# Where the second edge pass makes the own part of a message, and which banks it uses

## The reference, cut to what matters

```
def f(W1, W2, W3):
    tp = (x_src[:, :, None] * edge_sh[:, None, :]).reshape(n_edges, d * s)
    out1 = jnp.concatenate([x_src, tp], axis=-1)
    out2 = _mlp(edge_inv, W1, W2, W3)
    return out1 * out2
...
edge_v = f(Wv1, Wv2, Wv3)
edge_v = edge_v.reshape(n_edges, H, F // H) * jnp.sqrt(jax.nn.relu(alpha))[:, :, None]
node_out = jax.ops.segment_sum(edge_v, edge_dst, num_segments=n_nodes)
return node_out @ W_out
```

## Time and profile before

| | us |
|---|---|
| median of 3 runs | 4718.47 (4709.61 to 4720.08) |
| the profiled execution, its own time | 4691.75 |
| its span, first to last instruction | 4690.0 |
| busy, PE / DVE / ACT / POOL | 3424.4 / 3775.0 / 2138.1 / 1853.7 |
| granted TensorE clock, mean over the span | 0.885 |

### The profile page before, as it was taken

One profiled execution on the slowest core, in us unless ns is written; L12 is line 12 of the kernel. 1 busy time (PEld: TensorE's weight loads), 2 busy tenths in 40 slices (PEclk: granted clock), 3 DMA queues, 4 the chain that ended last, 5 costly groups with the idle time before them and its releaser, 6 DMA issues. The chain is left out here.

```text
span 4690.0 us, 65792 instructions
## 1 busy us (share of the span) xinstructions
PE 3424.4 (73%) x20105; PEld 1508.5 (32%) x20105; DVE 3775.0 (80%) x6298; ACT 2138.1 (46%) x4386; POOL 1853.7 (40%) x3682
## 2 busy tenths in 40 slices
PE   5665653465688888888888089999999999248157
PEld 2111111111233343333333034444444444112122
DVE  8999995898566666666666878888888888599898
ACT  6999991674233333333333033444434443047066
POOL 0100445000655555555554056666666666200000
PEclk9989885677899999999999589999999999579589
DMA  4754999663344444444443023333333333356445
GB/s 174 303 223 162 313 326 317 219 210 113 99 120 116 113 115 113 115 113 112 117 114 104 4 78 94 91 93 93 91 94 91 93 93 88 127 176 227 158 177 184
DMA packets 373210, 675.89 MB, mean 144 GB/s; under 512 B 74684, under 2 KB 274940, under 8 KB 361216
## 3 DMA queue, kind: packets, MB, share of 16 engines
q1 hardware_dynamic: 308752, 569.80, 37.0%
q0 software_dynamic: 39568, 78.78, 6.8%
q10 hardware_dynamic: 24544, 23.10, 1.7%
HBM read 399.80 MB, written 271.65 MB: 143 GB/s over the span
## 5 line engine op out<-in xcount | busy, mean ns | idle before, releaser
L734 POOL DMA_INDIRECT arena<-h_table,srci x808 | 772.5, 956 | 596.3 <-issue 244.2
L1751 DVE TENSOR_TENSOR arena<-banks,arena 128x1024 f32<-128x1024 f32 x404 | 493.6, 1222 | 262.9 <-remote 162.9
L829 PE MATMUL banks<-arena 128*128 128x500 bf16 x1440 | 411.4, 416 | 273.9 <-DVE arena L1474 211.4
L1871 DVE TENSOR_TENSOR arena<-banks,arena 128x512 f32<-128x512 f32 x808 | 518.8, 684 | 36.5 <-PE banks L1036 13.0
L1879 DVE TENSOR_TENSOR arena<-banks,arena 128x512 f32<-128x512 f32 x808 | 516.9, 681 | 1.3 <-PE banks L1042 1.3
L1166 ACT ACTIVATE arena<-arena,h 128x128 bf16<-128x128 f16 x1440 | 465.1, 416 | 61.0 <-DVEq L1390 40.9
L1318 ACT ACTIVATE arena<-banks 64x256 f32<-64x256 f32 x808 | 306.3, 379 | 341.2 <-PE banks L1068 334.2
L931 PE MATMUL banks<-arena 128*64 128x256 f32 x3232 | 451.2, 402 | 0.0
L1056 PE MATMUL banks<-arena 128*64 128x256 f32 x3232 | 438.5, 392 | 0.5 <-DVE arena L1881 0.5
L1042 PE MATMUL banks<-arena 64*128 64x512 f32 x1616 | 436.2, 617 | 1.2 <-DVE arena L1879 0.9
L1462 DVE TENSOR_SCALAR arena<-arena,agg 128x500 bf16<-128x500 f16 x1440 | 413.3, 362 | 0.2
(11 more groups left out here) (296 smaller groups left out, 6422.5 us busy)
## 6 DMA issues: line engine op xcount, KB each, us to landing
arena<-c_flat SPq DMA_DIRECT2D x75, 1562.5 KB, 6.8
slots<-arena SPq DMA_DIRECT2D x90, 1000.0 KB, 3.8
arena<-hs_dump SPq DMA_DIRECT2D x404, 128.0 KB
arena<-mask_rows SPq DMA_DIRECT2D x50, 781.2 KB, 4.3
arena<-in_edge_attr SPq DMA_DIRECT2D x202, 128.0 KB
arena<-placed SPq DMA_DIRECT2D x202, 128.0 KB
xs_dump<-arena SPq DMA_DIRECT2D x202, 128.0 KB
hs_dump<-arena SPq DMA_DIRECT2D x202, 128.0 KB
```

The lines of the kernel that those rows point to most:

```text
L734: pool.indirect_dma_start(out=xs[par][:, k * D:(k + 1) * D], out_offset=None, in_=h_table, in_offset=bass.IndirectOffsetOnAxis(ap=srci[:, ...
L829: last = pe.matmul(ps[4 + r % 2][:, 0:BW], row_hot[r][:, k * P:(k + 1) * P], col_hot[r][:, k * BW:(k + 1) * BW], start=k == 0, stop=k == K ...
L1751: V.tensor_tensor(bt_pair[i].rearrange("p (j n) -> p j n", j=2), banks[:, 5 * COLS:7 * COLS].rearrange("p (j n) -> p j n", j=2), h2k[t % 2 ...
L1871: V.tensor_tensor(dt_[j % 2], ps[3 + j % 2][:, :], xat[t % 3], ALU.mult).then_inc(dt_sb, 1)
```

## The change

The own part's two matmuls contract over 64 rows each, one in each row half of the array, with 128 output partitions, of which 64 are zero: the weights become block-diagonal. The first writes columns 256 to 511 of bank 1, the second those of bank 7, whose columns 0 to 255 take the messages turned back. In PE's order the own part moves from the end of the turn to just behind values 2 and 3, ahead of the transposes. DVE makes vt[4] by two instructions of 64 partitions instead of one of 128. Both engines get waits for the shared bank.

```diff
             def p2_own(t):
                 at(vt_sb, t * 5, pe)
-                for half in range(2):
-                    last = pe.matmul(ps[1][half * D:(half + 1) * D, 0:TW // 2], v3[4][:, 0:D],
-                                     hv[t % 2][:, half * (TW // 2):(half + 1) * (TW // 2)], start=True, stop=True)
+                at(msgr_sb, t - 1, pe)
+                for half, bank in enumerate((ps[1], ps[7])):
+                    rows = slice(half * D, (half + 1) * D)
+                    last = pe.matmul(bank[:, TW // 2:TW], v3[4][rows, :], hv[t % 2][rows, half * (TW // 2):(half + 1) * (TW // 2)], start=True, stop=True)
                 last.then_inc(y_ps, 1)
...
                 pe.wait_ge(msg_sb, t + 1)
                 at(msgr_sb, t, pe)
+                pe.wait_ge(vt_sb, t * 5 + 5)
                 for g in range(2):
                     last = pe.transpose(ps[7][:, g * P:(g + 1) * P], msgt[:, g * P:(g + 1) * P], ident)
...
                     for j in (2, 3):
                         p2_value(t - 1, j)
+                    p2_own(t - 1)
                 if t + 1 < T:
                     p2_turned(t + 1)
...
                     p2_message(1).then_inc(half_ps, 1)
-                    p2_own(t - 1)
...
             ran(V.tensor_copy(out=v3[4][0:D, 0:D], in_=wv3n[0:D, 0:D]))
+            ran(V.tensor_copy(out=v3[4][D:P, D:P], in_=wv3n[D:P, 0:D]))
             ran(V.memset(v3[4][D:P, 0:D], 0.0))
+            ran(V.memset(v3[4][0:D, D:P], 0.0))
...
-                    V.tensor_tensor(vt[4], ps[1][:, 0:TW // 2], x0t[t % 3], ALU.mult).then_inc(vt_sb, 1)
+                    at(msgr_sb, t, dve)
+                    V.tensor_tensor(vt[4][0:D, :], ps[1][0:D, TW // 2:TW], x0t[t % 3][0:D, :], ALU.mult)
+                    V.tensor_tensor(vt[4][D:P, :], ps[7][D:P, TW // 2:TW], x0t[t % 3][D:P, :], ALU.mult).then_inc(vt_sb, 1)
```

## The result

The changed kernel took 5048.71 us (median of 4, 5046.61 to 5050.53) against 4715.66 us before on the same chip: a ratio of 1.0707, 95% interval 1.0688 to 1.0726, or 333 us more. The forecast was 4996, the range 4950 to 5075. The profiled execution took 5049.14 us, its span is 5047.4. It is 357 us longer than the profiled one of before; 25 of these lie ahead of the second pass, where nothing was changed: the first vt[4] starts at 2749.7 us, in the profile of before at 2725.0. The comparison on one chip, above, gives 333.

A forecast was written before the change was run, and what follows sets the result against it. The prediction took a 6.30 us loop through DVE and PE as the bound; the new loop 2.53 + 1.06 + 0.43 + 2.93 + 0.06 + 0.68 = 7.69 us adds 278 us, giving 4996 us, range 4950 to 5075.

The forecast's parts named there:

- DVE's new wait: DVE can start vt[4] only after ACT's copy out of bank 7, closing a loop of 7.69 us a turn.
- the term of 2.93: From PE's first transpose to the end of ACT's copy out of bank 7: 2.93 us, nothing in it shrinks.
- The own part's matmuls: On PE behind values 2 and 3: 0.43 us, bounds 0.32 and 0.54, weight loads hidden behind matmuls.
- Rival B: PE's own pair not side by side or its loads not hidden: about 0.86 us, 86 us more, 5082; chance 0.05.
- DVE's second instruction: The two vt[4] instructions on DVE take 0.68 us together, or 0.76 if the second costs its full 0.42.
- The release: From the end of ACT's copy out of bank 7 to DVE's start of vt[4]: 0.06 us.
- The likeliest case's own range: Bounds of the whole kernel's time for the 0.86-chance forecast, with 10 us of scatter: 4964 to 5047 us.
- Its new place: Own part on PE ahead of the transposes: these start 0.43 us later, messages 0 and 1 end as before.
- Rival A: Own part off the loop, DVE never waits for the copy, PE binds: 28 us gain, 4690; chance 0.04.
- the 6.16 us: PE's turn in the second pass without its wait of about 0.14 us: it could do 6.16.
- Rival C: PE's new waits in the second pass lower its clock for 10 turns: 46 us more, 5042; chance 0.04.
- Rival D: No change: DVE's wait ends where its vt[4] starts today, needing ACT's copy 1 us earlier; chance 0.01.

The follow-up runs named there:

- e1: The changed kernel with ACT's copy of the message turned back moved ahead of its copies of the turned rows: 1.0025 of before, 4701.52 us.
- e3: The kernel before the change with only vt[4] made by two DVE instructions of 64 partitions, both from bank 1: 1.0246 of before, 116 us more.
- e3c: The kernel before with vt[4] whole and a spare DVE product on partitions 0 to 63 behind it: 4748.87 us against 4690.66 before, one execution.
- e3d: The kernel before with vt[4] whole and a spare DVE product on partitions 64 to 127 behind it: 4805.49 us against 4690.66 before, one execution.
- e5: The changed kernel with DVE's new wait moved behind the first half of vt[4], so only the second half waits: 1.0470 of before.
- e2: The changed kernel with the message turned back handled first on both PE and ACT: 0.9988 of before, 6.27 us a turn.
- e4: The kernel before with the own part, unchanged in form, moved behind values 2 and 3: 1.0047 of before, 6.43 us a turn.
- e8: The kernel before with the own part, unchanged in form, moved behind messages 2 to 4: 0.9899 of before, 4665.41 us against 4711.40.

## Why the prediction was right, and where it was off

*DVE's new wait decides.* Right, and shown: the term of 2.93 came out at 2.92, DVE idles 2.10 us for L1330 in 199 tiles (about 1.9 forecast), and e1, which leaves the wait and moves what it waits for, takes the turn to 6.35. e1's turn had been worked out from the same terms.

*The own part's matmuls cost 0.43 with hidden weight loads.* Right: from values to transposes 1.49 as forecast. The first loads of L1050 run while the values stream through the same rows, here in the timeline of weight loads, then the second step of the values in that of PE:

```profile
3407.64 0.19 PEld L1050 LDWEIGHTS banks<-arena 64*128 64x128 f32 x2 [0.24 <-issue]
3408.07 0.19 PEld L1050 LDWEIGHTS banks<-arena 64*128 64x128 f32 x2 [0.24 <-issue]
```

```profile
3407.64 0.60 PE L1042 MATMUL banks<-arena 64*128 64x512 f32 x2
```

The second step of the values starts at 3407.64, and the own part's start at 3408.07 follows it by the usual 0.43. Rival B is out for this shape, and so is the first of the two rules that the prediction quotes from the Trainium skill (TensorE: Matmul & The Clock Gate, Part 3, The mechanism), that a load overlaps a running matmul only where its row group differs.

*DVE's second instruction.* This term of the sum was mis-sized: 0.68 forecast, 0.89 measured, 42 of the 56 us. The step said that 64 partitions instead of 128 change no column count. That is true and beside the point; e3, e3c and e3d show that the start partition costs, 0.09 for the instruction that changes it and 0.12 for the one that changes back. The Trainium skill has this rule, which the prediction did not weigh: by "VectorE: DVE Perf Modes", section "Two Vector instructions with no wait between them", an instruction starts only when all earlier ones have finished if an input begins in another quadrant of 32 partitions than the first input that the last instruction reading that memory took from it, or its output in another than the last output into that memory. With that rule the traces agree wherever such an instruction stands (the changed kernel, e3, e3d), and e3c, which has none, shows 0.34.

*The release.* 0.06 forecast, 0.13 measured, 14 us. It was taken from other pairs of engines (PE to DVE, ACT to POOL); the traces have 0.13 from ACT to DVE in the changed kernel and in e1 (3408.09 to 3408.22), 0.04 in e5, and why is open.

*The likeliest case's own range*, 4964 to 5047, missed the 5048.71 by 2 us, by these two terms; the range of the whole held it, and its upper end had been raised for rivals B and C, not for them.

*Its new place.* The step that messages 0 and 1 end at the same time as before is wrong. From the start of values 2 and 3 to their end it was 2.78 us (3408.46 to 3411.24) and is 3.31 now (3407.11 to 3410.42), longer by the own part ahead of them; it is the next basis that comes at the same time (3.32 before). The sum didn't use the step.

*Rival A and the 6.16 us.* Its condition, a copy a turn old, was not met, as argued. But its price was wrong, 28 us and a turn of 6.16: the step that PE "could do 6.16" once the loop of 6.30 is cut overlooked the second loop, 0.42 + 2.49 + 0.05 + 3.31 = 6.27 (e2). The rows of before show it, as basis at 3405.48 and DVE's rows at 3405.93, 0.45 later and only 0.03 above its minimum. So moving the own part ahead of the transposes could have won 0.03 us a turn at best, 6 us: even without its wait the change had next to nothing to gain there.

*Rival C, the clock.* The granted clock stayed 1.00 in the repeating turns, with PE idle for 1.57 us of 7.97. Its price of 46 us stood on one stretch of the first pass with a clock of 0.96; the five other full stretches of 200 us show 0.93 to 0.95, which would make it up to 80. Rival D had nothing for it.

## What to carry to other kernels

Before an instruction gets a new wait, write down where in the same turn its releaser stands, on its own engine's queue too: here a bank shared by DVE's and ACT's reads tied DVE to the last of ACT's six copies behind the transposes, and swapping the order of the copies gave back 1.62 of 1.67 us. In a pipeline of turns list every closed loop, not only the one that binds: one 0.03 us behind it decides what cutting the first is worth, and a piece of work is moved for gain only out of both. Splitting an elementwise instruction into halves by partitions cost 0.55 us a tile here where its columns would have cost 0.34 (e3), since the second half starts at another partition than its neighbours.

## What the runs showed of the hardware that was not expected

- DVE's products in a row overlap by about 0.08 us; with a change of the start partition from 0 to 64 or back they don't: 0.34 us against 0.43 and 0.46 for 256 columns (e3c, e3d).
- From the end of ACT's copy to the DVE instruction that it releases: 0.04 us in e5, where that instruction asks for this semaphore alone, 0.13 in the changed kernel and in e1, where it asks for three others first. What makes the difference isn't shown.
- A column-half matmul pair placed between row-half and full-array ones cost 0.15 us more than a row-half pair at the same place (e4), and the same pair behind other column-half matmuls nothing more (e8: 0.53 to the next basis, 0.54 at its old place).
